# One-hot tiles turned by a plain float32r product with gate columns beside the identity, and expert sums scattered to token rows

## What is computed

```
tok  = x.reshape(-1, 128)                      # 1024 tokens
gate = softmax(tok @ Wgate.T)                  # 1024 x 8 experts
vals, idx = top_k(gate.T, 128)                 # each expert takes its 128 best tokens
g = layernorm(tok[idx]) * mlp_g + mlp_b
y = gelu(g @ fc1s[e].T + b1s[e]) @ fc2s[e].T + b2s[e]
tok = tok.at[idx].add(y * vals)                # added back at the tokens' rows
```

## Time and profile before

| what | us |
|---|---|
| median of 3 runs | 396.5 (395.57 to 396.94) |
| the profiled execution's own time | 395.64 |
| its span, first to last instruction | 393.9 |
| TensorE matmul busy | 365.6 (93%) |
| TensorE weight load busy, beside the matmuls | 260.2 (66%) |
| ScalarE busy | 267.2 (68%) |
| VectorE busy | 256.0 (65%) |
| GpSimd busy | 148.6 (38%) |

### The profile page before, as it was taken

How to read it: one execution, slowest core, us unless ns; L and a number is a source line. 1 busy time by engine, 2 the same in 40 slices (tenths; PEclk the granted TensorE clock), 3 DMA queues, 4 the chain that set the end, 5 groups by cost and what they waited for, 6 DMA issues and landing times.

```text
span 393.9 us, 8921 instructions
## 1 busy us (share of the span) xinstructions
PE 365.6 (93%) x3188; PEld 260.2 (66%) x3188; DVE 256.0 (65%) x596; ACT 267.2 (68%) x656; POOL 148.6 (38%) x157
## 2 busy tenths in 40 slices
PE   7998997679999999999999999999999776899995
PEld 7586676346766766766766766666655555588894
DVE  3757356668677667767767767767777368790423
ACT  3355656688878878878878999878877255357331
POOL 5200233464565465465465465485451020000000
PEclk9999999999999999999999999999999955589999
DMA  4900000003910000000000000000000000000001
GB/s 122 279 3 2 2 2 0 0 2 89 342 54 2 2 2 2 2 1 2 2 0 3 2 2 2 2 1 2 2 2 1 2 2 0 2 0 2 0 2 53
DMA packets 7519, 9.76 MB, mean 25 GB/s; under 512 B 379, under 2 KB 4278, under 8 KB 7478
## 3 DMA queue, kind: packets, MB, share of 16 engines
q1 hardware_dynamic: 5654, 7.11, 6.0%
q10 hardware_dynamic: 1824, 2.10, 1.8%
HBM read 8.68 MB, written 0.52 MB: 23 GB/s over the span
## 4 chain that ended last, share of the span: by engine, by line
PE 83%; DVE 7%; ACT 5%; issue 2%; POOL 1%; DVEq 0%; POOLq 0%; ACTq 0%
PE bank L1352 15%; PE pair L1303 8%; PE pair L1279 7%; PE bank L1303 7%; PE bank L1081 7%; PE bank L1319 6%; PE pair L1319 4%; PE bank L1330 4%; PE bank L1207 2%; PE bank L1499 2%; PE pair L1089 2%; PE pair L1081 2%; PE pair L1339 2%; PE pair L1215 2%; PE pair L1421 1%
## 5 line engine op out<-in xcount | busy, mean ns | idle before, releaser
L415 POOL TENSOR_TENSOR qk_rstd<-qk_ms,minus_half 128x8 f32<-128x8 f32 x32 | 52.4, 1639 | 99.0 <-DVE qk_ms L870 99.0
L1319 PEld LDWEIGHTS bank<-ident,probs 64*128 64x128 f32 x512 | 36.9, 139 | 46.7 <-issue 46.5
L1352 PE MATMUL bank<-probs_T,v_s 128*64 128x256 f32 x512 | 62.3, 385 | 0.6 <-DVE x_att L913 0.6
L882 DVE TENSOR_REDUCE negmax<-pair 128x1 f32<-128x512 f32 x64 | 43.8, 686 | 21.3 <-PE pair L1303 21.3
L594 ACT ACTIVATE probs_T<-bank 128x512 f32<-128x512 f32 x64 | 37.9, 593 | 24.3 <-PE pair L1319 24.1
L585 ACT ACTIVATE probs<-pair,negmax 128x512 f32<-128x512 f32 x64 | 43.8, 685 | 9.3 <-DVE negmax L882 8.4
L1319 PE MATMUL bank<-ident,probs 64*128 64x64 f32 x512 | 43.4, 225 | 2.4 <-DVE probs_T L890 1.3
L1352 PEld LDWEIGHTS bank<-probs_T,v_s 128*64 128x64 f32 x512 | 34.1, 136 | 16.6 <-issue 0.8
L1319 PE MATMUL pair<-ident,probs 64*128 64x64 f32 x512 | 44.9, 228 | 0.0
L890 DVE COPY probs_T<-pair 128x512 f32<-128x512 f32 x64 | 43.6, 681 | 1.2 <-PE pair L1319 1.2
L585 ACT ACTIVATE probs<-bank,negmax 128x512 f32<-128x512 f32 x64 | 43.5, 692 | 0.1
(11 more groups left out here) (262 smaller groups left out, 766.2 us busy)
## 6 DMA issues: line engine op xcount, KB each, us to landing
fc_raw<-in_L_cond_fc2s_dram SPq DMA_DIRECT2D x1, 2048.0 KB, 15.0
x_in<-in_x_dram ACTq DMA_DIRECT2D x1, 512.0 KB, 3.9
w<-in_L_cond_mlp_w_dram SPq DMA_DIRECT2D x2, 256.0 KB, 4.8
wout<-in_L_cond_Wout_dram SPq DMA_DIRECT2D x1, 512.0 KB
b_all<-in_L_cond_b2s_dram SPq DMA_DIRECT2D x1, 512.0 KB, 11.5
out_dram<-final SPq DMA_DIRECT2D x2, 256.0 KB, 2.4
film<-in_L_cond_film_w_dram SPq DMA_DIRECT2D x2, 128.0 KB, 4.2
wq<-in_L_cond_q_w_dram SPq DMA_DIRECT2D x1, 64.0 KB, 2.8
```

The source lines that it names most:

```text
L415: pool.tensor_tensor(qk_rstd[:, p % 2, :, :].rearrange("p c t -> p (c t)"), qk_ms[:, p % 2, :, :].rearrange("p c t -> p (c t)"), minus_hal ...
L882: dve.tensor_reduce(negmax[:, t % 2, h:h + 1], bank[2 * (t % 2) + h][:, :], AX, ALU.max, negate=True)\
L1319: last = pe.transpose(bank[(4, 6)[q]][:, n * HD:n * HD + HD], probs[rows, t % 2, n // NC, n % NC * P:n % NC * P + P], ident[rows, rows])
L1352: last = pe.matmul(bank[5][h * HD:h * HD + HD, 0:2 * P], v_s[:, m % 4, k, h * HD:h * HD + HD], probs_T[:, r % 2, h, k, :], start=(k == 0), ...
```

## The change

- The eight transposes per chunk become eight plain float32r products: the one-hot tile is stationary, and the moving operand is the new tile `turner`, with the identity in 128 columns and the gate's high and low parts in 16 more, 144 in all. Each result thus has the turned tile and, beside it, each slot's weight as far as this chunk holds it. Three experts go to one bank (the last group has two), and two sets of three banks alternate between the chunks. Turning runs one chunk behind gathering.
- ScalarE makes three copies per chunk for the first seven chunks, VectorE three for the last. `onehot_T` keeps the 144 columns.
- `slot_weights`, `copy_weights`, `turn_weights` and `join_weights` go. VectorE sums the gate columns in `slot_weight`, one small reduction per expert.
- GpSimd fills the identity columns of `turner` once, early in the kernel.
- `scatter` has the turned one-hot tile stationary (one of 8 per expert) and the 256 columns of `y_parts`, high and low part side by side, moving. The sums have tokens on partitions, two chunks to a bank in four banks. The closing copies and transposes go; VectorE adds `x_att`, the high and the low sums in two additions of 256 columns per bank, and the first output DMA waits for two banks, the second for four.

```
+        turner = keep("turner", [P, TC, P + 2 * E], F32R)
...
-        onehot_T = moe("onehot_T", [P, E, TOK], F32R)
-        y_hi = Area(area_start)("y_hi", [P, E, D], F32R)
-        y_lo = Area(area_start + 4 * E * D)("y_lo", [P, E, D], F32R)
+        onehot_T = moe("onehot_T", [P, E, TC, P + 2 * E], F32R)
+        y_parts = Area(area_start)("y_parts", [P, E, 2, D], F32R)
...
+        HOT_PARTS = ((0, 3), (3, 6), (6, 8))
+        def hot_bank(c, n):
+            return bank[((5, 6, 7), (3, 4, 0))[c % 2][n]][:, 0:3 * (P + 2 * E)].rearrange("p (e n) -> p e n", e=3)
+        def sum_bank(n):
+            return bank[(5, 6, 7, 0)[n]]
...
-                sp.wait_ge(final_ready, half + 1)
+                sp.wait_ge(final_ready, 2 * half + 2)
...
+            pool.tensor_scalar(turner[:, :, 0:P], ident[:, :].unsqueeze(1).to_broadcast([P, TC, P]), 1.0, None, ALU.mult)\
+                .then_inc(turner_set, 1)
...
-            for c in range(TC):
-                if c == TC - 1:
-                    for q in range(2):
-                        act.wait_ge(xg_done, q + 1)
-                        act.activation(xg[:, 4 * q:4 * q + 4, :].rearrange("p e n -> p (e n)"),
-                                       bank[1 + q][:, :], ACT.Identity, bias=col("mlp_b"),
-                                       scale=col("mlp_g")).then_inc(xg_ready, 1)
-                for q in range(2):
-                    act.wait_ge(hotT_done, 2 * c + q + 1)
-                    act.activation(onehot_T[:, 4 * q:4 * q + 4, c * P:c * P + P],
-                                   bank[5 + q][:, :].rearrange("p (e n) -> p e n", e=4), ACT.Copy)\
+            def copy_hot(c):
+                for n, (lo, hi) in enumerate(HOT_PARTS):
+                    act.wait_ge(hotT_done, 3 * c + n + 1)
+                    act.activation(onehot_T[:, lo:hi, c, :], hot_bank(c, n)[:, 0:hi - lo, :], ACT.Copy)\
                        .then_inc(hotT_copied, 1)
+            for c in range(TC - 2):
+                copy_hot(c)
+            for q in range(2):
+                act.wait_ge(xg_done, q + 1)
+                act.activation(xg[:, 4 * q:4 * q + 4, :].rearrange("p e n -> p (e n)"), bank[1 + q][:, :],
+                               ACT.Identity, bias=col("mlp_b"), scale=col("mlp_g")).then_inc(xg_ready, 1)
+            copy_hot(TC - 2)
             for e in range(E):
                 act.wait_ge(fc1_done, e + 1)
                 wait(act, fc2_done, e - 1)
...
                     last = act.activation(ug[:, e % 2, c, :], bank[1 + e % 2][:, c * CAP:c * CAP + CAP],
                                           ACT.Gelu_apprx_tanh, bias=col("b1s", e * DC + c))
                 last.then_inc(gelu_done, 1)
-            act.wait_ge(sum_done, 1)
-            act.activation(sum_T[:, 0:N], bank[7], ACT.Copy).then_inc(sum_copied, 1)
...
+            gate_parts = turner[:, :, P:P + 2 * E].rearrange("p c (e k) -> p c e k", k=2)
+            link(dve.tensor_copy(gate_parts[:, :, :, 0], gate[:, :, :]))
+            dve.tensor_tensor(gate_parts[:, :, :, 1], gate[:, :, :], gate_parts[:, :, :, 0].bitcast(F32), ALU.subtract)\
...
-            def copy_weights(q):
...
-            def join_weights(q):
...
-            copy_weights(0)
+            def slot_weight(e):
+                at = slice(P + 2 * e, P + 2 * e + 2)
+                dve.tensor_reduce(w_slot[:, e:e + 1], onehot_T[:, e, :, at].bitcast(F32), mybir.AxisListType.XY, ALU.add)\
+                   .then_inc(wslot_ready, 1)
+            for n, (lo, hi) in enumerate(HOT_PARTS):
+                dve.wait_ge(hotT_done, 3 * (TC - 1) + n + 1)
+                dve.tensor_copy(onehot_T[:, lo:hi, TC - 1, :], hot_bank(TC - 1, n)[:, 0:hi - lo, :])\
+                   .then_inc(hotT_last, 1)
+            dve.wait_ge(hotT_last, 3)
+            dve.wait_ge(hotT_copied, 3 * (TC - 1))
             for e in range(E):
-                if e % (E // 2) == 0:
-                    join_weights(e // (E // 2))
+                slot_weight(e)
+            dve.wait_ge(wslot_ready, E)
+            for e in range(E):
                 dve.wait_ge(fc2_done, e + 1)
                 link(dve.tensor_tensor(y_sum[:, e % 2, :], b2_all[:, e, :], bank[3 + e % 2][:, 0:D], ALU.add))
-                link(dve.tensor_scalar(y_hi[:, e, :], y_sum[:, e % 2, :], w_slot[:, e:e + 1], None, ALU.mult))
-                dve.scalar_tensor_tensor(out=y_lo[:, e, :], in0=y_sum[:, e % 2, :], scalar=w_slot[:, e:e + 1],
-                                         in1=y_hi[:, e, :].bitcast(F32), op0=ALU.mult, op1=ALU.subtract)\
+                link(dve.tensor_scalar(y_parts[:, e, 0, :], y_sum[:, e % 2, :], w_slot[:, e:e + 1], None, ALU.mult))
+                dve.scalar_tensor_tensor(out=y_parts[:, e, 1, :], in0=y_sum[:, e % 2, :], scalar=w_slot[:, e:e + 1],
+                                         in1=y_parts[:, e, 0, :].bitcast(F32), op0=ALU.mult, op1=ALU.subtract)\
                    .then_inc(y_ready, 1)
-                if e == 1:
-                    copy_weights(1)
-            dve.wait_ge(sum_done, 2)
-            dve.wait_ge(sum_copied, 1)
-            dve.tensor_copy(sum_T[:, N:TOK], bank[5][:, :]).then_inc(sum_copied, 1)
-            for half in range(2):
-                dve.wait_ge(sumT_done, half + 1)
-                dve.tensor_tensor(final[:, half * NC:half * NC + NC, :], x_att[:, half * NC:half * NC + NC, :],
-                                  bank[1 + half][:, :].rearrange("p (c d) -> p c d", d=D), ALU.add)\
-                   .then_inc(final_ready, 1)
+            for n in range(NC):
+                dve.wait_ge(sum_done, n + 1)
+                at = slice(2 * n, 2 * n + 2)
+                sums = sum_bank(n)[:, :].rearrange("p (c k d) -> p c k d", c=2, k=2)
+                link(dve.tensor_tensor(final[:, at, :], x_att[:, at, :], sums[:, :, 0, :], ALU.add))
+                dve.tensor_tensor(final[:, at, :], final[:, at, :], sums[:, :, 1, :], ALU.add).then_inc(final_ready, 1)
...
             pe.wait_ge(fcT_copied, 2 * E - 2)
-            for c in range(TC):
+            pe.wait_ge(gate_split, 1)
+            pe.wait_ge(slots_ready, 1)
+            pe.wait_ge(turner_set, 1)
+            def gather(c):
                 pe.wait_ge(hot_dve, c + 1)
                 for q in range(2):
                     for n, part in enumerate((tn_hi, tn_lo)):
...
                                          start=(c == 0 and n == 0), stop=(c == TC - 1 and n == 1))
                     if c == TC - 1:
                         last.then_inc(xg_done, 1)
-                for q in range(2):
-                    if c:
-                        pe.wait_ge(hotT_copied, 2 * c - 1 + q)
-                    turn4(bank[5 + q], [onehot[:, c, 4 * q + e, :].bitcast(F32) for e in range(4)])\
-                        .then_inc(hotT_done, 1)
-            pe.wait_ge(gate_split, 1)
-            pe.wait_ge(slots_ready, 1)
-            def slot_weights(q, chunks):
...
-            def turn_weights(q):
...
+            def turn_hot(c):
+                if c == 1:
+                    pe.wait_ge(fcT_copied, 2 * E)
+                for n, (lo, hi) in enumerate(HOT_PARTS):
+                    wait(pe, hotT_copied, 3 * (c - 2) + n + 1)
+                    for e in range(lo, hi):
+                        last = pe.matmul(hot_bank(c, n)[:, e - lo, :], onehot[:, c, e, :], turner[:, c, :],
+                                         start=True, stop=True)
+                    last.then_inc(hotT_done, 1)
+            for c in range(TC):
+                gather(c)
+                if c:
+                    turn_hot(c - 1)
+            turn_hot(TC - 1)
             def up(e):
                 if e < 2:
-                    pe.wait_ge(xg_ready, 2)
+                    pe.wait_ge(xg_ready, e + 1)
                 wait(pe, gelu_done, e - 1)
                 for c in range(DC):
                     last = pe.matmul(bank[1 + e % 2][:, c * CAP:c * CAP + CAP], fc1_T[:, e, c * P:c * P + P],
...
             def down(e):
                 pe.wait_ge(gelu_done, e + 1)
+                if e < 2:
+                    pe.wait_ge(hotT_last, e + 1)
                 wait(pe, y_ready, e - 1)
                 for c in range(DC):
                     last = pe.matmul(bank[3 + e % 2][:, 0:D], ug[:, e % 2, c, :], fc2_T[:, e, c, :],
...
             def scatter(e):
                 if e == 0:
-                    pe.wait_ge(hotT_copied, 2 * TC)
+                    pe.wait_ge(hotT_copied, 3 * (TC - 1))
+                    pe.wait_ge(hotT_last, 3)
                 pe.wait_ge(y_ready, e + 1)
-                for b, dst in enumerate((bank[7], bank[5])):
-                    for n, part in enumerate((y_hi, y_lo)):
-                        last = pe.matmul(dst[:, :], part[:, e, :], onehot_T[:, e, b * N:b * N + N],
-                                         start=(e == 0 and n == 0), stop=(e == E - 1 and n == 1))
-                    if e == E - 1:
+                for c in range(TC):
```

(63 more changed lines are left out.)

## The result

The changed kernel takes 391.61 us (median of 4 runs, 391.26 to 391.85) against 396.5 us before; the ratio is 0.990, with a 95% interval of 0.987 to 0.993. It is faster by 1%. The forecast was 392.7 us with a change of -3.8 us. The profiled execution took 391.85 us, its span 390.1 us against 393.9: -3.8 us. Two later series of the same kernel gave 391.24 and 391.02 us beside 395.5 and 394.9 us for the kernel before.

A forecast was written before the change was run, and what follows sets the result against it. TensorE was taken to bound gather, turn and the experts' loop. -11.76 + 7.49 + 0.33 - 0.14 + 0.28 = -3.80 us gives 391.8 profiled, 392.7 us median; own range 391.6 to 393.9, whole range 390.3 to 398.0.

The forecast's parts named there:

- transposes and slot weights' road removed: TensorE loses 64 transposes (6.99 us), slot weights' products (3.71) and the restarts around turning them (1.06): 11.76 us less.
- 64 turning products: Turning by float32r products of 144 columns, priced at 0.117 us each: 7.49 us more, with ends at 4.2 and 16.0.
- seam before the first down: Down(0) now directly follows up(1) and waits for gelu(0): a TensorE stall of 0.33 us.
- scatter, seven experts on the chain: Scatter by 64 products of 256 columns instead of 32 of 512, at 0.114 us each: 0.14 us less.
- end: From the last scatter's start to the last addition's end: 3.88 instead of 3.60 us, 0.28 more, with eight VectorE additions.
- last output DMA: After the last addition: the output DMA keeps its place and its 2.87 us stay.
- The bound: In gather, turn and the experts' loop TensorE is always busy, so each of its instructions added or removed counts in full.
- Rival A: Turning: narrow float32r is slow, 0.250 us per product, 16.0 instead of 7.49 us, kernel at 401.2 us; chance 0.20.
- B: Turning is cheaper than the load rows say, 0.081 us per product, kernel at 390.7 us; chance 0.09.
- GpSimd's filling: Early in the kernel, one instruction fills the identity columns, hidden in GpSimd's idle time; were it not, some 2.4 us.
- The forecast of the median: Whole kernel: the runs' median lies 0.86 us above the profiled execution, forecast at 391.8, so 392.7 us.

The follow-up runs named there:

- 168-column run: The changed kernel with 168 instead of 144 moving columns in each of the 64 turning products; 391.21 us, ratio 0.989.
- 16-column runs: The changed kernel with each turning product split into a transpose and a 16-column float32r product: alternating 397.8 us, a bank's transposes first 398.21 us.

## Why the prediction was right

| step | predicted us | in the trace us | from |
|---|---|---|---|
| transposes and slot weights' road removed | -11.76 | -11.76 |, groups gone after |
| 64 turning products | +7.49 | +6.99 | first gather to up(0): 14.90 after, 15.13 before, 0.24 of it clock |
| seam before the first down | +0.33 | +0.65 | 3.32 less 3 x 0.89 |
| scatter, seven experts on the chain | -0.14 | +0.15 | down(0)'s end to last down's end: 17.32; before 20.08 less 2.91 removed (1.85 + 2 x 0.34 + 0.20 + 0.18) |
| end | +0.28 | +0.18 | 3.78 and 3.60 |
| last output DMA | 0 | -0.13 | 2.74 and 2.87 |
| clock and what comes before the first gather | 0 | +0.11 | 0.35 late, 0.24 made up |
| sum | -3.80 | -3.81 | |

**The bound and what was removed** were right: TensorE's groups followed each other without gaps, and each group removed came off in full. The experiment that removes only the slot weights' road shows that this one step is nearly all of the gain: 3.55 of 3.90 us in the part of the trace behind the last gather.

**Turning** was the open price, between 0.066 and 0.250 us. It is 0.109 to 0.111 us, just under the 0.111 to 0.124 of the rows that I argued from. The argument was that a 144-column product is paced by its load; the 168-column run, which changes nothing, and the 16-column runs, which pay 0.11 us behind a product and 0.085 behind a transpose for hardly any stream, bear it out as far as the stream goes. Rival A, a narrow float32r product at float32's pace, did not happen; nor did B. With the load's figure in the Trainium skill, page "TensorE: Matmul & The Clock Gate", section "LDWEIGHTS (loading the stationary operand)", a load of 128 columns is estimated at 128/1.2 = 107 ns whatever the contraction, which agrees with the 0.109 to 0.111 us measured; that transposes, whose load record is shorter, have the same pace is not explained by it.

**The seam** was found in advance but at half its size: the wait was 0.33 us as priced, but I left out that the group behind a wait restarts 0.27 us slower. The same restart stood in rows that I used, 1.09 against 0.89.

**Scatter** was taken at 0.114 us per product and is 0.119, the upper row (half of a 512-column product). The step said 0.14 us less (for eight experts) and it is 0.15 more (for the seven on the chain).

**The end** and GpSimd's filling were nearly as forecast, 3.78 us for 3.88 and 2.78 us, hidden, for 2.4; additions that do not depend on the one before overlap it by some 0.08 us (0.34 instead of 0.42), which I had left out.

So it is luck that the total agrees to 0.01 us: the forecast was 0.5 us too dear for turning and 0.3 us too cheap for the seam and for the scatter each, and these and small errors cancel; the single steps were good to about 0.3 to 0.5 us. The forecast of the median was not as near: 392.7 us against 391.61, at the lower end of its own range of 391.6 to 393.9. It took the changed kernel's median 0.86 us above its profiled execution, as in the old one, and it was 0.24 below. That the runs' median fell by 4.9 us and the profiled span by 3.8 is within the runs' spread: the interval of the ratio is -2.9 to -5.1 us, and later series have -4.3 and -3.9.

## What to carry to other kernels

Where float32r products need a new 128 x 128 stationary tile each time, they cost 0.11 us each here, with 128, 144 and 168 moving columns alike. So look for a small product with the same stationary tile and put its columns beside those of the large one: here 16 gate columns rode for nothing, and as products of their own they cost 5.4 us in the trace. When a filler leaves the chain, look for what it hid, and move an independent group into the gap; price a wait with its restart. A rearrangement that only moves work from TensorE's end to VectorE's, as the scatter to token rows does, should be tried by itself before it is kept.

## What was not expected of the hardware

A float32r product of 16 columns begins 0.11 us after another product but 0.08 to 0.09 after a transpose, so that between transposes it adds only about 0.085 us. In scatter products with 256 moving columns the pace was 0.119 us and with 128 columns 0.111, so the second 128 columns add less than a tenth. The granted clock fell and rose at different times in executions of the same kernel (0.50, 0.62 or 0.78 on average from 317 to 319 us), which moved the span of the changed kernel between 389.3 and 391.0 us with the work behind it equally long.
